# Rolling the batch loop of two stages of an attention and nearest-neighbour kernel into a counted loop on each engine

## The chip, the cores and the metric

The kernel runs on one core of a Trainium2 chip. The metric is the device time of one execution in microseconds. The engines are TensorE (PE; its weight loads are listed as PEld), VectorE (DVE), ScalarE (ACT), GpSimd (POOL) and SyncE (SP), which here only issues DMAs. Each engine has an instruction stream of its own, and they meet only through semaphores.

## The reference

Two layers run on 32 batches of 128 channels by 1024 positions.

```python
# layer 0: attention in chunks of 64 positions, 8 heads of 16 channels
q, k, v = ctx @ Wq.T + bq, ctx @ Wk.T + bk, ctx @ Wv.T + bv
out = softmax(q k^T * Dh**-0.5 + mask) v, projected by W_out, times masks, plus x
y = (out - mean) * rsqrt(var + 1e-5)              # over the 1024 positions
# layer 1: 30 nearest neighbours of each position by the first three rows of ctx
idx = top_k(2 p.p - |p|^2 - |p|^2, 30)
rel = pts[idx] - pts                              # then rho, theta, phi
h = three small linear layers with batch norm over all pairs and leaky relu
att = softmax(h, over the 30 neighbours)
result = y + sum_k y[:, idx_k] * att_k
```

(The distance in the kernel is taken over all 128 rows of ctx, as the reference's call does.)

## The kernel before

The program has three stages, each a block of its own with an all-engine meeting point at its end.

**Stage A** (`stage_a`) loops over the 32 batches. For each it takes 8 tiles of 128 positions. PE makes the distances (`pd_ps`, lines 413 and 415), ACT moves them into a ring of four tiles in SBUF (`pd_sb`), and DVE finds the 32 largest of each row in four rounds: MAX8 (line 891) finds eight, FIND_INDEX8 (line 896) their places, and MATCH_REPLACE8 (line 898) takes them out, except in the last round. Two tiles are interleaved, so that an operation on one follows an operation on the other. Beside that, PE, ACT and POOL do the chunked attention of the same batch (`s_ps`, `sS`, `kz`, `mi_ps`) and gather the coordinates of the neighbours of the batch before by products with one-hot rows: a `fill` (line 488) spreads an index code, ACT turns it into a one-hot row `ohT`, and twelve small products (line 509) fetch the coordinates. There are 60 such units for each batch. PE works two tiles ahead of DVE with the distances and one tile ahead with the scores.

**Stage B** works on the whole set of 7680 pairs a partition (spherical features, the three small layers, the batch norms). It has no loop over batches.

**Stage E** loops over the 32 batches again. Each batch has two halves (`q`, with n = 2b + q), and each half has eight groups of 16 rows. For each group DVE makes one-hot rows `e_oh` (line 1835), PE multiplies them by spread weights into `e_a_ps` (line 1907, 48 products of 32 columns), ACT copies that into `e_at` (line 1678), and PE multiplies the `e_at` of the half before by the turned rows `e_xT` into `e_o_ps` (line 1921, two products behind each group from the second on, four behind that one). DVE adds `e_o_ps` to the normalised rows (line 1822). At the head of each half PE turns the rows of the next half (line 1886), and DVE needs ACT's copy of them for `heat` (line 1791).

The order of the instructions is written out by hand in an `emit` function on each engine, which takes the batch `b`, the pair number `j` = b // 2, the parity `par` = b % 2 and two flags for the ends. Semaphores are never reset within a stage: a wait names a running total, such as `b * UNITS + q * K + k + 1`. `gate` (line 105) is a wait that is an instruction of its own, as it also counts up a semaphore; each MAX8 and each FIND_INDEX8 stands behind one or two of them. `batches` calls `emit` for each batch; it is the only thing that the change touches. In both stages it hands over plain numbers, so that all totals and addresses are constants and the program has the instructions of all 32 batches one behind the other.

```python
            for b in range(B):
                emit(b, b // 2, b % 2, b == 0, b == B - 1)
```

Of the kernel before, what the change touches and what calls it, by code (L numbers as in the profile page):

```python
# [23 lines left out]
B, C, T = 32, 128, 1024  # L24
# [123 lines left out]
def stage_a(nc, x, ctx, mask, w_in, b_in, w_out, b_out, consts, y_dram, cst, con, planes, idx_all, stats_all, sums, wts, weights):  # L148
    OHR = 3
    XR = 97  # L150
    with ExitStack() as st:
# [146 lines left out]

        def batches(eng, emit):

            for b in range(B):
                emit(b, b // 2, b % 2, b == 0, b == B - 1)

        block = st.enter_context(nc.Block())

# [1 line left out]
        def _(sp):  # L307
# [36 lines left out]
            def emit(b, j, par, first, last):  # L344
# [15 lines left out]
                sp.dma_start(y_dram[b], y_s[:].rearrange("p h t -> p (h t)")).then_inc(y_stored, 16)  # L360

            batches(sp, emit)
            sp.wait_ge(y_stored, 16 * B)
            sp.wait_ge(weights_landed, 9 * 16)

        @block.tensor
        def _(pe):
# [214 lines left out]
            queries_keys(misc0, 0, 0)  # L582
            scores(0, 0, 0)
            batches(pe, emit)
            tail = Misc(TAIL, TAIL % 2)
            probs_in = turn_probs(tail, B - 1, TILES - 1)
# [5 lines left out]
        def _(act):  # L592
# [163 lines left out]
            for t in range(2):  # L756
                for h in range(2):
                    distances(0, 0, t, h, normed)
            queries_keys(mv0, 0, 0)
            batches(act, emit)  # L760
            tail = Moves(TAIL, TAIL % 2)
            turned_probs(tail)
# [753 lines left out]
def stage_e(nc, con, planes, idx_all, stats_all, last_bn, y_dram, out):  # L1516
# [5 lines left out]
    with ExitStack() as st:  # L1522
# [71 lines left out]

        def batches(eng, emit):

            for b in range(B):
                emit(b, b // 2, b % 2, b == B - 1, b < B - 2)


        block = st.enter_context(nc.Block())
# [1 line left out]
        @block.sync  # L1603
        def _(sp):
            def load(b, par):

                if passed(b - 1):
                    gate(sp, x1_ready, b - 1, e_sp_gates)
                sp.dma_start(y_s[:, par, :], y_dram[b]).then_inc(y_landed[par], 16)

            def store(b, q):
                gate(sp, o_added, b * QUADS + q + 1, e_sp_gates)
                sp.dma_start(out[b][:, bass.ts(q, HALF)], o_s[:, q, :]).then_inc(stored[q], 16)

            def emit(b, j, par, last, further):
                if not last:
                    load(b + 1, 1 - par)
                if passed(b):
                    store(b - 1, 1)
                store(b, 0)  # L1620

            load(0, 0)
            batches(sp, emit)
            store(B - 1, 1)
            for q in range(QUADS):
                sp.wait_ge(stored[q], 16 * B)

        @block.scalar
        def _(act):
# [76 lines left out]
            logits(1)  # L1706
            exponent(1)
            batches(act, emit)

        @block.vector  # L1710
        def _(dve):
# [160 lines left out]
            for step in range(4):  # L1872
                soft(1, step)
            batches(dve, emit)
            add(B * QUADS - 2, B - 1, 0, 1)
            add(B * QUADS - 1, B - 1, 1, 1)
# [94 lines left out]
```

## Time and profile before

| | |
|---|---|
| median of 3 runs | 5462.31 us (5458.58 to 5465.13) |
| the profiled execution | 5458.58 us, of which the span is 5456.7 us |
| busy over the span | DVE 96%, PE 79%, ACT 71%, POOL 46% |
| stage A | from the start to about 3912 us, with a tail from about 3650 us on that has no loop |
| stage B | about 3912 to 4230 us |
| stage E | about 4230 us to the end |
| mean granted TensorE clock | 0.91 of full speed |

A busy share is the time in which an engine had an instruction in work. An engine that is nearly always busy in a stage sets that stage's time; idle time of another engine is slack as long as its work is there when it is needed. The time outside the span is 1.9 us.

### The profile page before, as it was taken

What the parts mean: (1) busy time and instruction counts of PE and PEld (TensorE: products, weight loads), DVE (VectorE), ACT (ScalarE), POOL (GpSimd) and SP (SyncE); (2) the same over time, 40 slices, a digit from 0 to 9 for tenths busy, and PEclk for the clock granted to TensorE, in tenths of its full rate; (3) what the DMA queues carried; (4) which work ended last, traced back from release to release, by engine and by line L of the source; (5) the groups of instructions that cost most, each with busy time, mean ns of one, the idle gap of its engine ahead of it and who ended that gap; (6) DMA issues with size and microseconds to landing.
All of it is one profiled execution on the core that took longest, in us unless ns stands there. A gap on an engine that the chain in (4) does not pass through costs nothing. (4 is left out here: it accounts for less than half of the span.)

```text
span 5456.7 us, 152862 instructions
## 1 busy us (share of the span) xinstructions
PE 4292.5 (79%) x62610; PEld 2634.9 (48%) x63182; DVE 5235.3 (96%) x7660; ACT 3871.1 (71%) x9296; POOL 2502.9 (46%) x3044
## 2 busy tenths in 40 slices
PE   5777787877777777777777777773295899999999
PEld 2444444444444444444444444442142677777776
DVE  7999999999999999999999999998998999999997
ACT  3677777777777777777777777776433777777776
POOL 3566676666766667666676666664000000000000
PEclk7899998999999999999999999996597899999999
DMA  1000000010000100001000010000000001000010
GB/s 32 17 26 23 17 17 17 17 33 17 17 17 17 33 17 17 17 17 32 17 17 17 17 33 17 17 9 5 0 0 0 32 28 32 30 32 32 28 34 26
DMA packets 135464, 112.55 MB, mean 21 GB/s; under 512 B 105328, under 2 KB 105840, under 8 KB 134640
## 3 DMA queue, kind: packets, MB, share of 16 engines
q1 hardware_dynamic: 134768, 102.73, 6.5%
q8 instruction: 502, 8.22, 0.6%
q14 instruction: 194, 1.59, 0.1%
HBM read 69.16 MB, written 33.55 MB: 19 GB/s over the span
## 5 line engine op out<-in xcount | busy, mean ns | idle before, releaser
L594 ACT ACTIVATE ohT<-oh_ps 128x512 bf16<-128x512 f32 x1920 | 1151.5, 615 | 163.0 <-PE oh_ps L488 130.1
L896 DVE FIND_INDEX8 idx<-vals,pd_sb 128x8 uint16<-128x1024 f32 x1024 | 1258.9, 1234 | 0.0
L891 DVE MAX8 vals<-pd_sb 128x8 f32<-128x1024 f32 x1024 | 1209.2, 1227 | 42.3 <-ACT pd_sb L594 42.1
L509 PEld LDWEIGHTS g_ps<-tparts,ohT 128*128 128x128 bf16 x23040 | 857.3, 98 | 358.4 <-issue 109.3
L898 DVE MATCH_REPLACE8 pd_sb<-vals,pd_sb 128x1024 f32<-128x1024 f32 x768 | 942.4, 1227 | 0.0
L509 PE MATMUL g_ps<-tparts,ohT 128*128 128x24 bf16 x23040 | 873.8, 174 | 86.6 <-issue 36.8
L1907 PEld LDWEIGHTS e_a_ps<-planes,e_oh 120*128 120x128 bf16 x24576 | 684.3, 97 | 269.6 <-issue 169.1
L733 ACT ACTIVATE sS<-s_ps,mx 128x64 f32<-128x64 f32 x2048 | 612.7, 327 | 278.8 <-DVE mx L915 278.8
L1678 ACT COPY e_at<-e_a_ps 128x512 f32<-128x512 f32 x512 | 543.9, 1062 | 302.7 <-PE e_a_ps L1907 295.7
L1907 PE MATMUL e_a_ps<-planes,e_oh 120*128 120x32 bf16 x24576 | 699.7, 177 | 58.7 <-DVE e_oh L1835 58.7
L488 PE MATMUL oh_ps<-bitsT,code 128*128 128x512 bf16 x1348 | 568.4, 426 | 216.2 <-ACT bitsT L751 127.2
L413 PE MATMUL pd_ps<-ctx_s 128*128 128x512 f32 x1024 | 616.7, 686 | 88.4 <-ACT pd_sb L594 86.5
L1113 POOL TENSOR_TENSOR sS<-sS,rs 128x512 f32<-128x512 f32 x256 | 266.7, 1042 | 808.4 <-DVE rs L919 808.3
L1835 DVE TENSOR_TENSOR e_oh<-e_pairs,e_iotan 120x2048 bf16<-120x2048 bf16 x512 | 625.6, 1223 | 0.9 <-PE e_a_ps L1907 0.9
L1040 POOL TENSOR_TENSOR gsb<-gsb 128x240 f32<-128x240 f32 (+2 forms) x1152 | 559.6, 486 | 90.3
L1137 POOL TENSOR_TENSOR kz<-kt,cst 128x1024 f32<-128x1024 f32 x256 | 486.8, 1902 | 153.3 <-ACT kt L594 146.1
L488 PEld LDWEIGHTS oh_ps<-bitsT,code 128*128 128x128 bf16 x1920 | 188.2, 101 | 757.4 <-ACT ohT L594 311.0
L1921 PE MATMUL e_o_ps<-e_at,e_xT 128*128 128x512 f32 x1024 | 548.3, 628 | 0.2 <-ACT e_at L1678 0.2
L594 ACT ACTIVATE pd_sb<-pd_ps,nxx 128x512 f32<-128x512 f32 x512 | 365.0, 713 | 207.9 <-PE pd_ps L415 207.6
L1037 POOL TENSOR_TENSOR gsb<-gsb,hi1h 128x480 f32<-128x480 f32 x384 | 442.9, 1153 | 67.3 <-ACT gsb L675 67.3
L446 PE MATMUL s_ps<-xp,negs 32*64 32x512 bf16 x512 | 113.9, 441 | 427.8 <-ACT sS L733 421.1
L733 ACT ACTIVATION_READ_ACCUMULATOR sS<-s_ps,mx 128x1 f32 x2048 | 450.1, 220 | 0.0
(277 smaller groups left out, 6700.6 us busy)
## 6 DMA issues: line engine op xcount, KB each, us to landing
ctx_s<-in_ctx SPq DMA_DIRECT2D x32, 512.0 KB, 4.9
maskb<-in_mask_Bx1x_ff SPq DMA_DIRECT2D x32, 512.0 KB, 6.3
x_s<-in_x SPq DMA_DIRECT2D x32, 512.0 KB, 5.7
y_spill<-y_s SPq DMA_DIRECT2D x32, 512.0 KB, 3.0
e_y<-y_spill SPq DMA_DIRECT2D x32, 512.0 KB, 4.1
out<-e_o SPq DMA_DIRECT2D x64, 256.0 KB, 2.5
table<-in_ctx SPq DMA_DIRECT2D x96, 4.0 KB, 5.9
pd_sb<-in_shape_constants SPq DMA_DIRECT2D x1, 1024.0 KB, 5.2
```

The lines of the kernel that those rows point to most:

```text
L413: nc.tensor.matmul(pd_ps[:], ctx_s[:, par, bass.ts(t, P)], ctx_s[:, par, bass.ts(h, HALF)], start=True, stop=False)
L488: nc.tensor.matmul(oh_ps[k % 2][:], code[:, k % KT, :], bitsT[:, k // KT, :], start=True, stop=True).then_inc(oh_ready, 1)
L509: m = nc.tensor.matmul(found_ps[gi % 2][:, k % GK, t, :], ohT[:, k % OHR, bass.ts(t, P)], tparts[:, par, part, :], start=(part == 0), stop ...
L594: return nc.scalar.activation(dst, src, func, scale=scale, bias=bias)
L733: m = nc.scalar.activation(sS[:, t % 2, hd, :], s_ps[:, hd, :], ACT.Exp, bias=mx[:, t % 2, hd:hd + 1], accum_out=rs[:, t % 2, hd:hd + 1])
L891: nc.vector.max(vals[:, i, :], pd_sb[:, (t + i) % RING, :]).then_inc(topk_step, 1)
L896: found = nc.vector.max_index(idx16[:, par, t + i, 8 * r:8 * r + 8], vals[:, i, :], work)
L898: nc.vector.match_replace(work, vals[:, i, :], work, REMOVED).then_inc(topk_step, 1)
L1040: steps(nc.gpsimd.tensor_tensor(sums[:, :, 0:width], sums[:, :, 0:width], sums[:, :, width:2 * width], ALU.add))
L1835: v.tensor_tensor(oh[pp, g % RING], low.to_broadcast([QCOLS, NB // 2, LO, 2]), row.to_broadcast([QCOLS, NB // 2, LO, 2]), ALU.is_equal).th ...
L1907: m = nc.tensor.matmul(a_ps[g % 2][:, i].rearrange("p t e -> p (t e)"), oh[pp, g % RING, i // 2, :, i % 2], spr[q][pp, part, :, (g * NB + ...
L1921: m = nc.tensor.matmul(o_ps[q][:], xT[:, par, e, :], at[:, q, e].rearrange("p t n -> p (t n)"), start=(e == 0), stop=(e == HI - 1))
```

## The change

Both `batches` functions keep the first two and the last two batches as they were, and put the 28 between them into a counted loop (`Fori`) of 14 passes on each engine, with two batches in its body. The body's `b` is now 2j or 2j + 1 with j in a register, so wherever `emit` computes a total to wait for, or an address with `b` in it, the value is worked out from the register while the program runs. Tile parities stay constants. Where `emit` or a helper of it asks whether `b` is a plain number (for the first batches, where there is nothing to wait for yet), a register counts as "not a plain number". At the end of each pass every engine adds one to its own counter, compares and branches back; no engine waits there for another, and no hint for the fetching of the branch's target is given. The instructions of the engines, their order, the buffers and the DMAs are the same.

```diff
@@ stage_a
         def batches(eng, emit):
 
-            for b in range(B):
-                emit(b, b // 2, b % 2, b == 0, b == B - 1)
+            emit(0, 0, 0, True, False)
+            emit(1, 0, 1, False, False)
+            with eng.Fori(1, B // 2 - 1) as j:
+                emit(j * 2, j, 0, False, False)
+                emit(j * 2 + 1, j, 1, False, False)
+            emit(B - 2, B // 2 - 1, 0, False, False)
+            emit(B - 1, B // 2 - 1, 1, False, True)
@@ stage_e
         def batches(eng, emit):
 
-            for b in range(B):
-                emit(b, b // 2, b % 2, b == B - 1, b < B - 2)
+            emit(0, 0, 0, False, True)
+            emit(1, 0, 1, False, True)
+            with eng.Fori(1, B // 2 - 1) as j:
+                emit(j * 2, j, 0, False, True)
+                emit(j * 2 + 1, j, 1, False, True)
+            emit(B - 2, B // 2 - 1, 0, False, False)
+            emit(B - 1, B // 2 - 1, 1, True, False)
```

## Rows read from the trace of the kernel before

**Rows 1.** Busy time of each engine by stretch: stage A, stage E, one batch of each.

```profile
core 0: us, PE busy (x) PEld busy (x) DVE busy (x) ACT busy (x) POOL busy (x), PEclk, DMA share, GB/s
120.00:3650.00 3530.00, 2756.91 (x34389) 1592.86 (x34936) 3508.11 (x5220) 2646.02 (x7844) 2368.28 (x2901) 0.91 0.07 20
4300.00:5300.00 1000.00, 960.55 (x21758) 716.08 (x21754) 916.99 (x1515) 749.29 (x801) 0.00 (x0) 1.00 0.09 31
...
1523.90:1638.30 114.40, 88.64 (x1104) 51.41 (x1122) 113.60 (x171) 85.92 (x255) 77.57 (x95) 0.91 0.08 20
4733.60:4771.20 37.60, 36.14 (x819) 26.92 (x818) 34.50 (x57) 28.14 (x31) 0.00 (x0) 1.00 0.09 31
```

**Rows 2.** Waits in stage E, 4300 to 5300 us: us in total, times, longest.

```profile
PE e_a_ps L1907 <- DVE e_oh L1835: 39.5, 54, 1.0
```

**Rows 3.** The page: instructions in all, and the DMA queues.

```profile
PE 4292.5 (79%) x62610; PEld 2634.9 (48%) x63182; DVE 5235.3 (96%) x7660; ACT 3871.1 (71%) x9296; POOL 2502.9 (46%) x3044
...
q8 instruction: 502, 8.22, 0.6%
q14 instruction: 194, 1.59, 0.1%
```

**Rows 4.** DMA issues: size and us from issue to landing.

```profile
y_spill<-y_s SPq DMA_DIRECT2D x32, 512.0 KB, 3.0
...
cst<-in_shape_constants SPq DMA_DIRECT2D x1, 294.0 KB, 2.9
...
bias<-in_L_xattn_b_out SPq DMA_DIRECT2D x1, 0.5 KB, 5.0
```

**Rows 5.** DVE in order of time at the end of a batch of stage A.

```profile
1636.01 2.33 DVE L891 MAX8 vals<-pd_sb 128x8 f32<-128x1024 f32 x2
1638.26 0.07 DVE L896 MATCH_VALUE_LOAD idx<-vals,pd_sb 128x8 f32 x1
1638.32 1.22 DVE L896 FIND_INDEX8 idx<-vals,pd_sb 128x8 uint16<-128x1024 f32 x1
```

**Rows 6.** Instructions of the sequencers, by line: duration min/median/max in ns.

```profile
L108 DVEq EVENT_SEMAPHORE  x2334: 21/21/21569, 11.7 to 3712.9; - x195
```

```profile
L1904 PEldq EVENT_SEMAPHORE  x510: 51/51/51, 4250.5 to 5442.5; - x170
```

```profile
L1207 DVEq COMPARE_BRANCH  x1: 57/57/57, 4229.1 to 4229.1; - x1
```

**Rows 7.** PE in order of time around the end of a batch of stage E (at 4733.62).

```profile
4731.46 1.37 PE L1907 MATMUL e_a_ps<-planes,e_oh 120*128 120x32 bf16 x48
4732.68 1.10 PE L1921 MATMUL e_o_ps<-e_at,e_xT 128*128 128x512 f32 x2
4733.62 0.44 PE L1886 MATMUL e_pr_ps<-e_identb,e_rowsb 128*120 128x128 bf16 x5
4733.90 1.36 PE L1907 MATMUL e_a_ps<-planes,e_oh 120*128 120x32 bf16 x48
4736.29 1.37 PE L1907 MATMUL e_a_ps<-planes,e_oh 120*128 120x32 bf16 x48 [1.02 <-DVE e_oh L1835]
```

**Rows 8.** DVE in order of time over the same end of a batch.

```profile
4731.44 0.83 DVE L1810 TENSOR_SCALAR planes<-e_wgt,cst 120x1024 bf16<-120x1024 bf16 x2
4732.18 1.22 DVE L1835 TENSOR_TENSOR e_oh<-e_pairs,e_iotan 120x2048 bf16<-120x2048 bf16 x1
4733.82 0.69 DVE L1822 TENSOR_TENSOR e_o<-e_o_ps,e_x 128x512 f32<-128x512 f32 x1 [0.42 <-PE e_o_ps L1921]
...
4735.01 1.22 DVE L1835 TENSOR_TENSOR e_oh<-e_pairs,e_iotan 120x2048 bf16<-120x2048 bf16 x1
```

## Prediction, made before the changed kernel ran

> **What bounds the kernel now.** I read the busy time by stretch first. In stage A DVE is busy 3508 of 3530 us, 99.4%, while in one batch of 114.4 us PE idles 25.8 us, ACT 28.5 us and POOL 36.8 us [rows 1]. So DVE sets stage A, and whatever makes DVE's queue run dry there is paid in full, while the other three have slack. In stage E it is the other way round: PE is busy 960.6 of 1000 us and DVE 917.0 [rows 1]. PE sets stage E, and nearly all of what it waits for is DVE's one-hot rows, 39.5 us in 54 waits over 1000 us [rows 2]. Stage B and the tail of A have no loop over batches; the change leaves them alone.
>
> Then I looked at what feeds the engines. The page lists DMA queues of the kind "instruction": 502 packets with 8.22 MB and 194 with 1.59 MB [rows 3]. 8.22 MB over 62,610 matmuls and 63,182 weight loads is 65 bytes each, so the first queue carries PE's program in blocks of 16.4 KB, some 250 instructions. The other carries the rest in blocks of 8.2 KB, about 128 instructions at the same size. The programs are thus read in while they run. In a straight program the next block is always known; at a branch back it is an old one.
>
> **The size of a pass.** One batch of stage A has 1104 + 1122 instructions on PE, 171 on DVE, 255 on ACT, 95 on POOL; one of stage E has 819 + 818 on PE, 57 on DVE, 31 on ACT [rows 1]. A pass is two batches, so its body is about 18 PE blocks in A and 13 in E, and on DVE 342 instructions and its gates in A (2334 gates over 32 batches are 73 a batch [rows 6]), some 490 or four blocks, against about one in E. Fori(1, 15) makes 14 passes, so each loop has 13 taken branches on each engine.
>
> **What a taken branch costs.** No taken branch back stands in the trace. The compare-and-branch itself is small: one took 57 ns [rows 6]. What matters is whether its target must be fetched again. A block's packet keeps a DMA engine for 0.6% x 16 x 5456.7 / 502 = 1.04 us [rows 3], which is the lower bound of a fetch. The upper one is the slow read of 0.5 KB, 5.0 us from issue to landing [rows 4]. I take 3.0 us, after the plainest single transfers, 2.9 and 3.0 us [rows 4].
>
> The Trainium skill ("Runtime: NRT & Kernel Launch", section Instruction fetch mechanics) says that a taken branch whose target isn't in the instruction memory forces a fetch before anything goes on, and that PE holds 2048 instructions, the others 512. By that rule PE misses in both stages, DVE and ACT can miss in A, and the small bodies of E and of POOL need not. The trace agrees with the blocks of 16 KB for PE, not for the other queue, whose blocks are 8.2 KB; whether a block is kept, no row here shows.
>
> **Term 1, DVE in stage A.** The branch can be covered only by work already queued. The gate ahead of the last FIND_INDEX8 opens when the second MAX8 ends, at about 1638.3; from there DVE has two finds of 1.22 us [rows 5], 2.4 us in all, and the last one's issue takes some 0.2 us of that, so 2.2 us cover the branch. Against it stand 3.0 us of fetch and about 0.5 us for counter, compare, and the waits at the head of the next batch with their register values (a gate is 21 ns, a branch 57 ns [rows 6]; the register instructions are not in the trace). The stall is 1.3 us, times 13 = **16 us**. From both sides: 0 us (fetch 1.04), and (5.0 + 0.5 - 2.2) x 13 = 43 us. The branches of PE, ACT and POOL in stage A I cost at nothing: some 3 us every 229 us against a slack of 50 us or more on each; the distances are two tiles ahead of DVE in a ring of four. If that cover were gone they would cost up to 3 x 13 = 39 us.
>
> **Term 2, PE in stage E.** When PE's sequencer has issued the last group, the two products of line 1921 (0.94 us from 4732.68 to 4733.62) and part of the 48 pairs (1.22 us for all of them) are still ahead [rows 7]. How many are queued the trace doesn't show, so the cover is 0.94 to 2.2 us; I take 1.7. The stall is 3.0 + 0.3 - 1.7 = 1.6 us. Some of it comes back: in the second group after the boundary PE waits 1.02 us for `e_oh` [rows 7], because DVE's add at 4733.82 had waited for PE, and `e_oh` at 4735.01 stands behind it [rows 8]. During the stall DVE gets that done, unless its own branch, which stands ahead of the `e_oh` at 4732.18, holds it up. I count half of the 1.02 us. 1.1 us x 13 = **14 us**. From both sides: 0, and (5.0 + 0.3 - 0.94) x 13 = 57 us. Behind a stalled PE stand turn_pairs, ACT's copy and DVE's `heat`; they shift with PE and add nothing of their own.
>
> **Term 3, the arithmetic for the waits.** By the code PE waits about 210 times a batch in stage A and 48 times in E (16 groups twice, 6 before line 1921, 4 and 4 at the heads, 2 for the turning). Each value now comes from a register. The trace has no such instruction; the nearest row is a semaphore instruction on PE's sequencer, 51 ns [rows 6]. In stage A one more of that a wait is 10.7 us a batch, under the 25.8 us of slack: nothing. DVE's operations of 1.2 us cover several such instructions each. In stage E 48 x 51 ns x 28 batches = 69 us if all of it shows, 0 if none does. Six groups of eight have the 0.94 us of line 1921 behind them, in which the sequencer has four instructions to issue and can run ahead. Only the heads (a quarter of the waits, 17 us) have no such cover, and there PE waits for DVE anyway. I take half, **9 us**. Dynamic addresses on SP's DMAs, on POOL's writes to `planes` and on ACT's logits lie on engines with slack in both stages; they cost nothing, at most what POOL's slack leaves.
>
> **Sum.** 16 + 14 + 9 = 39 us on the profiled execution's 5458.6 us gives 5497.6 us. The median of the runs is 3.7 us above that execution, so I predict 5501 us. What a measurement of this kernel can tell from no change is 0.2%, 11 us.
>
> **Rivals.**
> *It costs nothing.* If a block comes back in under 1.7 us, or is kept, DVE's 2.2 us and PE's 1.7 us cover it, and terms 1 and 2 vanish. For it: a packet is only 1.04 us long, and the sequencers are ahead at just these places. Against it: no transfer of this kernel lands in so little. Time 5462 to 5468 us. It decides from a fetch of 1.7 us down. The Trainium skill ("Advanced Engine Details and Errata", section Control Flow Timing) gives a compare-and-branch about 108 ns and nothing further; by that alone the branches would come to an estimated 3 us over both stages.
> *The arithmetic shows in stage E.* PE has no slack there, and if the sequencer isn't ahead of the array, each wait costs at least its 51 ns: +69 us with one instruction a wait, +138 us with two. With 30 us for the branches that is 5561 to 5630 us. For it: PE idles only 4% [rows 1]. Against it: the 0.94 us behind most groups.
> *PE becomes the bound of stage A.* Three instructions a wait, 0.153 us x 210 = 32 us a batch, pass its slack of 25.8 us by 6 us, times 28 = 177 us; with all else about 5700 us. It decides from 25.8 / 210 = 0.12 us a wait. Against it: much of the arithmetic falls into time in which PE waits for ACT anyway.
> *Faster.* A body small enough to be kept needs no fetches; only POOL's and SP's can be, and neither bounds. 5445 us at best.
>
> **Chances.** Forecast (5474 to 5550) 0.57; costs nothing 0.17, of which 0.01 falls on the faster side; arithmetic in E 0.16; PE bound in A 0.07; faster 0.03. The range 5464 to 5600 us takes in the forecast, most of the second case and three quarters of the third; it leaves out the last two. Faster by over 0.2% 0.03, within 0.2% 0.16, slower 0.81.
>
> **What would show it.** In the changed profile: DVE in stage A with a gap of about 1.3 us ahead of the MAX8 at the head of each second batch, 13 times, and no other new gaps; the time of a batch inside the loop as before, 114.4 us. In stage E a gap of 1 to 2 us on PE ahead of line 1886 in every second batch, a batch otherwise at 37.6 us. The instruction queues keep their size or grow a little. It would be wrong if the batches inside a pass themselves get longer (the arithmetic shows), if the waits of PE for ACT in stage A vanish and DVE waits for `pd_sb` or `s_ps` (PE is the bound), or if the gaps at the branches are absent, or 4 us and more.

## The result, and the profile after

The changed kernel takes 5558.80 us (median of 4 runs, 5556.25 to 5561.41) against 5461.78 us before: a ratio of 1.0177 [1.0160, 1.0196], 97 us slower. The forecast was 5501 us. The direction and the range (5464 to 5600) hold; the size is 2.5 times the forecast one.

I split the spans of the two profiled executions (5456.7 and 5560.9 us) by the starts of two operations. From DVE's first FIND_INDEX8 to its last, stage A's search, it is 3651.4 us before and 3673.4 after, +22.0. From the first `e_oh` to the last, stage E, it is 1190.1 and 1270.2 us, +80.1. What lies between grows by 1.4 us. So four fifths of the loss is in stage E, where I had put 23 of 39 us.

The page of the changed kernel, busy time and instruction queues [rows 3]:

```profile
span 5560.9 us, 167643 instructions
PE 4439.9 (80%) x63182; PEld 2657.8 (48%) x63182; DVE 5241.2 (94%) x7660; ACT 3864.8 (69%) x9296; POOL 2499.9 (45%) x3044
...
q8 instruction: 566, 9.27, 0.7%
q14 instruction: 320, 2.62, 0.2%
```

The busy time of DVE, ACT and POOL is as before to 0.2%; PE's is 147 us larger. Only 27 us of that lie in stage E (1159.4 us before, 1186.1 after), and they are, as will be seen, products that took longer. The rest lies in stage A and is mostly a matter of records: 572 products are missing from the trace of before, and the trace of e7 below, which has them all and whose stage A is that of before, shows 118 us more there, too. Over 60 more blocks came through PE's instruction queue, and 126 more through the other: something is fetched again. (A block of PE's queue holds some 250 instructions by [rows 3].)

The two loops' own instructions by line (duration min/median/max in ns), the first two from stage A, the others from E [rows 6]:

```profile
L303 DVEq COMPARE_BRANCH  x14: 55/63/63, 492.4 to 3486.8; - x14
L303 PEldq COMPARE_BRANCH  x14: 83/3820/4472, 494.6 to 3490.2; - x14
...
L1604 PEldq FUSED_REGOPS  x14: 59/59/64, 4343.2 to 5397.3; - x14
L1604 PEldq ALU_OP  x14: 32/32/32, 4419.7 to 5475.3; - x14
L1604 PEldq COMPARE_BRANCH  x14: 79/3702/3864, 4419.8 to 5475.4; - x14
```

PE's branch is recorded with the wait for its target inside it: 3.7 us in E, 3.8 in A, and 0.08 us the one time in 14 that it isn't taken. The other engines' branches are recorded as about 0.05 us, and the wait, if any, follows: in A the next instruction that DVE's sequencer takes after its branch at 1873.8 comes 2.8 us later, ACT's 2.6 to 3.8 and POOL's 2.6 to 2.9 us later, in E DVE's comes about 0.27 and ACT's about 0.24 us later. The Trainium skill ("Runtime: NRT & Kernel Launch", Instruction fetch mechanics) has it that a taken branch stalls for a fetch where the target is not held; the trace agrees for PE in both stages and DVE, ACT and POOL in A, while DVE and ACT in E, with small bodies, show no fetch. With the sequencers' own instructions counted, a pass has 643 recorded instructions on DVE, 787 on ACT and 428 on POOL in A, and 201 on DVE and 118 on ACT in E.

PE in order of time around one of these branches, the one at 4905.8 [rows 7]. In brackets stands the idle time before a group and what ended it; `issue` means that the engine waited for nothing that the profile shows, so its next instruction simply came late:

```profile
4906.05 1.10 PE L1931 MATMUL e_o_ps<-e_at,e_xT 128*128 128x512 f32 x2
4909.77 0.78 PE L1896 MATMUL e_pr_ps<-e_identb,e_rowsb 128*120 128x128 bf16 x5 [2.61 <-issue]
4910.35 1.06 PE L1917 MATMUL e_a_ps<-planes,e_oh 120*128 120x32 bf16 x32
4913.48 1.87 PE L1917 MATMUL e_a_ps<-planes,e_oh 120*128 120x32 bf16 x64 [2.08 <-issue]
4915.19 3.76 PE L1931 MATMUL e_o_ps<-e_at,e_xT 128*128 128x512 f32 x4
4918.75 1.42 PE L1917 MATMUL e_a_ps<-planes,e_oh 120*128 120x32 bf16 x48
```

From the start of the two products of line 1931 to the group behind the four it is 12.70 us; before it was 6.63 (4732.68 to 4739.31; the first rows of that stretch are in [rows 7], the last two are these):

```profile
4737.51 1.96 PE L1921 MATMUL e_o_ps<-e_at,e_xT 128*128 128x512 f32 x4
4739.31 0.86 PE L1907 MATMUL e_a_ps<-planes,e_oh 120*128 120x32 bf16 x28
```

The 6.07 us are made up as follows, each from start to start. The turning comes 2.78 us late. It takes 0.58 us for 0.28: +0.30. The two groups behind it take 4.84 us for 3.61: a second gap of 2.08 us, from which the standing wait for `e_oh` of 1.02 us, which has gone, comes off, and 0.17 us of slower products: +1.23. The four products of line 1931 take 3.56 us for 1.80: +1.76.

The granted clock of the same place (PEclk is the third column from the right, full speed is 1.00):

```profile
core 0: us, PE busy (x) PEld busy (x) DVE busy (x) ACT busy (x) POOL busy (x), PEclk, DMA share, GB/s
4902.00:4908.60 6.60, 5.16 (x108) 3.58 (x105) 5.83 (x13) 5.11 (x7) 0.00 (x0) 1.00 0.01 2
4908.60:4912.60 4.00, 1.64 (x37) 1.56 (x38) 2.86 (x5) 0.69 (x1) 0.00 (x0) 0.52 0.53 195
4912.60:4918.90 6.30, 5.42 (x72) 3.16 (x72) 6.30 (x12) 2.12 (x2) 0.00 (x0) 0.50 0.02 7
4918.90:4940.00 21.10, 20.66 (x497) 15.55 (x495) 15.03 (x23) 14.97 (x16) 0.00 (x0) 1.00 0.05 16
```

From 4908.8 on, inside the first gap, TensorE has its lower level, 1.2 GHz, for 10.2 us, and pays in whatever runs there. In the 13 places the four products take 2.6 to 3.55 us, 3.2 in the mean, 18 us in all over 1.80 each; that, and the smaller groups beside them, makes up the extra busy time of PE in E.

PE's longest waits in stage E, 4300 to 5400 us (us in total, times, longest) [rows 2]:

```profile
PE e_pr_ps L1896 <- issue: 33.1, 13, 2.7
PE e_a_ps L1917 <- issue: 29.7, 12, 4.0
PE e_a_ps L1917 <- DVE e_oh L1845: 28.5, 42, 1.1
```

The first gap stands there 13 times and the second 12 times, 62.8 us together; the thirteenth second gap, 2.6 us at 5401.7, lies past the window. A batch with a branch ahead of it takes 43.5 us in the mean, the other one of a pair 37.7; both took 37.6 before. 5.95 us x 13 = 77 us.

In stage A, DVE at the end of a pass [rows 5], and its waits from 494 to 3490 us, first after, then before:

```profile
1873.48 1.22 DVE L901 FIND_INDEX8 idx<-vals,pd_sb 128x8 uint16<-128x1024 f32 x1
1874.62 0.07 DVE L901 MATCH_VALUE_LOAD idx<-vals,pd_sb 128x8 f32 x1
1874.67 1.22 DVE L901 FIND_INDEX8 idx<-vals,pd_sb 128x8 uint16<-128x1024 f32 x1
1877.12 2.35 DVE L896 MAX8 vals<-pd_sb 128x8 f32<-128x1024 f32 x2 [1.22 <-issue]
```

```profile
DVE vals L896 <- issue: 17.2, 13, 1.5
DVE vals L896 <- ACT pd_sb L599: 13.5, 20, 1.3
```

```profile
DVE vals L891 <- ACT pd_sb L594: 14.0, 24, 1.1
```

There is the gap that was forecast: two finds cover the branch, and 1.2 to 1.5 us stick out, 13 times.

### The profile page after: what moved, and what is told of

The parts are those of the page before. It is cut to its first block and busy times, and to the rows that moved or that the text cites. A ratio compares the mean times of both kernels' runs of the same rounds, so it can differ in the third digit from the quotient of the medians.

```text
span 5560.9 us, 167643 instructions
## 1 busy us (share of the span) xinstructions
PE 4439.9 (80%) x63182; PEld 2657.8 (48%) x63182; DVE 5241.2 (94%) x7660; ACT 3864.8 (69%) x9296; POOL 2499.9 (45%) x3044
## 3 DMA queue, kind: packets, MB, share of 16 engines
q14 instruction: 320, 2.62, 0.2%
## 5 line engine op out<-in xcount | busy, mean ns | idle before, releaser
L901 DVE FIND_INDEX8 idx<-vals,pd_sb 128x8 uint16<-128x1024 f32 x1024 | 1245.1, 1219 | 0.0
L493 PE MATMUL oh_ps<-bitsT,code 128*128 128x512 bf16 x1920 | 811.1, 429 | 223.6 <-ACT bitsT L756 132.8
L903 DVE MATCH_REPLACE8 pd_sb<-vals,pd_sb 128x1024 f32<-128x1024 f32 x768 | 928.8, 1209 | 0.0
L418 PE MATMUL pd_ps<-ctx_s 128*128 128x512 f32 x1024 | 645.4, 716 | 77.9 <-ACT pd_sb L599 76.5
L1931 PE MATMUL e_o_ps<-e_at,e_xT 128*128 128x512 f32 x1024 | 568.2, 649 | 0.2 <-ACT e_at L1688 0.2
```

What stands on the lines that cost most here:

```text
L418: nc.tensor.matmul(pd_ps[:], ctx_s[:, par, bass.ts(t, P)], ctx_s[:, par, bass.ts(h, HALF)], start=True, stop=False)
L493: nc.tensor.matmul(oh_ps[k % 2][:], code[:, k % KT, :], bitsT[:, k // KT, :], start=True, stop=True).then_inc(oh_ready, 1)
L901: found = nc.vector.max_index(idx16[:, par, t + i, 8 * r:8 * r + 8], vals[:, i, :], work)
L903: nc.vector.match_replace(work, vals[:, i, :], work, REMOVED).then_inc(topk_step, 1)
L1931: m = nc.tensor.matmul(o_ps[q][:], xT[:, par, e, :], at[:, q, e].rearrange("p t n -> p (t n)"), start=(e == 0), stop=(e == HI - 1))
```

## The experiments

In each, a stage that isn't named is as in the changed kernel. "A as before" or "E as before" means that this stage's `batches` is the plain loop over all 32 batches. Ratios are to the kernel before on the same chip.

**Does the register arithmetic cost anything?** One pass for each `Fori`, so that all 14 pairs of batches are written out, each with its `b` from a register, and no branch is taken:

```diff
-            with eng.Fori(1, B // 2 - 1) as j:
+            for jj in range(1, B // 2 - 1):
+              with eng.Fori(jj, B // 2 - 1, B) as j:
```

> All 28 batches of each stage stand one behind the other again, each pair in a counted loop of its own that is left after one pass: 13 of the 14 pairs still work their wait values and addresses out of a register, and no branch is taken. Theory F (the cost is the fetching behind a taken branch, on TensorE in stage E two fetches in a row, then a lower clock): within 0.2% of before, at most +11 us, a batch of stage E at 37.6 to 37.7 us. Theory R (the register arithmetic holds TensorE up): most of the change's 97 us stays, +60 us or more.

Measured: 5461.70 us, 0.9995 [0.9986, 1.0004]. The time can't be told from before, so the loss is in the taken branches. In E the arithmetic is small, but not nothing: a batch takes 37.68 us for 37.58, and two of them 39 us. PE's waits there, 4300 to 5400 us, before and then e1:

```profile
PE e_a_ps L1907 <- DVE e_oh L1835: 42.8, 59, 1.0
PE e_a_ps L1919 <- DVE e_oh L1847: 44.9, 58, 1.1
```

The wait for `e_oh` at each boundary is 1.11 us for 1.02. It comes from DVE: its add into `e_o` starts 1.74 us after the `e_oh` ahead of it for 1.64, behind a register instruction of 46 ns that stands between PE's result and the add. e7 below, where PE has no register at all, has the same 1.74, 1.11 and 37.67 us.

**Which stage?** A rolled with E as before, and E rolled with A as before.

> Only stage A is rolled, stage E is as before. Theory F: DVE loses 1.2 us at each of 13 branches, 16 us, and a few us more where TensorE and ScalarE come late with a tile: +15 to +28 us. Theory R: stage A has slack on all engines but DVE, so no more than a few us: under +11 us. A rival of mine that the stages cost about the same would have +48 us.

> Only stage E is rolled, stage A is as before. In the changed kernel's trace every second batch of E is about 5.9 us longer, 13 times, so 77 us; but TensorE's loop head now stands at another place in its fetch block, since the program ahead of it is longer. Theory F with two fetches in a row: between +40 us (a whole block stands behind the head, one gap of about 2.5 us) and +90 us (the head near a block's end). Theory R: +75 us wherever the head is.

Measured: 5477.94 us, 1.0029 [1.0018, 1.0040], +13.5; and 5564.77 us, 1.0178 [1.0162, 1.0193], +100. The two are more than the change has together, and e3 lies above the +40 to +90 us expected. In e3 the stage E body begins at another place of its block. PE there:

```profile
4734.81 1.10 PE L1926 MATMUL e_o_ps<-e_at,e_xT 128*128 128x512 f32 x2
4739.26 0.78 PE L1891 MATMUL e_pr_ps<-e_identb,e_rowsb 128*120 128x128 bf16 x5 [3.35 <-issue]
4743.69 2.74 PE L1912 MATMUL e_a_ps<-planes,e_oh 120*128 120x32 bf16 x96 [3.64 <-issue]
4746.27 3.22 PE L1926 MATMUL e_o_ps<-e_at,e_xT 128*128 128x512 f32 x4
```

The second gap stands after 5 products here, where it stood after 37 in the changed kernel, and is 3.6 us where it was 2.1. So it isn't tied to an operation or a wait of the kernel.

**Is the second gap the block behind the target?** If PE gets only the block that holds the target, its length behind the target decides. E rolled, A as before, the head of PE's loop body placed at slot 0 or 232 of a block (the slot is an instruction's place in its block):

```diff
-            with eng.Fori(1, B // 2 - 1) as j:
+            with eng.bass.Fori(1, B // 2 - 1, engines=[eng.engine],
+                               head_slot={eng.engine: 0} if eng.engine == mybir.EngineType.PE else None) as j:
```

> Only stage E is rolled, and TensorE's loop head is put at slot 0 of a fetch block of 256, so that a whole block stands behind the branch's target. Theory F: the second gap behind each branch (2.1 us in the changed kernel, after 32 of 48 products of the first group) is gone and the clock falls less: an excess of 2.5 to 4 us for a branch, +33 to +52 us. A rival, that the second gap is a wait for DVE or ScalarE, has it unchanged: +75 us.

> As the kernel with only stage E rolled, but TensorE's loop head at slot 232 of its fetch block: 24 slots stand behind the branch's target before the next block. Theory F (the block after the target is a second fetch in a row, and its wait is the longer, the fewer instructions stand before it): a gap behind the first group's opening products, an excess of 6 to 8 us for a branch, +80 to +105 us, and over 25 us more than with the head at slot 0. A rival, that only the one fetch of the target counts and the head's place changed something else: the same +56 us as at slot 0.

Measured: slot 0 5520.44 us, 1.0103 [1.0088, 1.0119], +56; slot 232 5547.20 us, 1.0151 [1.0135, 1.0167], +82; the first is 4 us above its expected range. With slot 0, PE after a branch:

```profile
4721.79 0.78 PE L1892 MATMUL e_pr_ps<-e_identb,e_rowsb 128*120 128x128 bf16 x5 [3.36 <-issue]
4722.37 2.77 PE L1913 MATMUL e_a_ps<-planes,e_oh 120*128 120x32 bf16 x96
4724.98 2.85 PE L1927 MATMUL e_o_ps<-e_at,e_xT 128*128 128x512 f32 x4
```

The second gap is gone and 44 of e3's 100 us with it; the lower clock stays (96 and four products in 5.3 us for 4.2). With slot 232 the gap is back after some 9 products. In the three traces with a second gap (the changed kernel, e3 and e5) the instructions behind it start 3.1 to 5.5 us after the branch ends, as late as a fetch that starts with the branch's end. With slot 0 PE comes to that place only 5.9 us or more after the branch and waits for nothing.

**What if the target is fetched ahead?** Both stages as in the changed kernel, with an instruction at the head of each body that names the target of the branch at its end:

```diff
-            with eng.Fori(1, B // 2 - 1) as j:
+            with eng.bass.Fori(1, B // 2 - 1, engines=[eng.engine], hint_back_edge=True) as j:
```

> Both stages rolled as in the change, and each loop carries a hint for the fetch of its branch's target, set at the head of each pass. Theory F: the target's block is there when the branch comes, the branch is short on every engine, and the stall ahead of line 1886 and of DVE's MAX8 goes: 0 to +25 us over before, what is left being the block behind the target if the hint brings one block alone (up to 2 to 3.6 us for a TensorE branch in E, then +25 to +50 us). If the branches stay at 3.7 us, the hint doesn't work for so long a body and nothing is learned of the cost: +97 us.

Measured: 5470.09 us, 1.0006 [0.9997, 1.0015]. 93 of the 97 us are gone. The hint and the branch of PE in E:

```profile
L1604 PEldq BRANCH_PREFETCH_HINT  x14: 36/36/40, 4318.2 to 5305.6; - x14
L1604 PEldq COMPARE_BRANCH  x14: 88/354/364, 4393.6 to 5382.1; - x14
```

In E 3.7 us have become 0.35, in A 3.8 have become 1.8. DVE's next instruction in A comes 0.5 us after its branch for 2.8, its gaps there are gone, and it waits 7.7 us for `pd_sb` in the stretch where it waited 14.0 before. The block behind the target still comes late (0.91 us of `issue` after 36 products at 4702.5), about where the wait for `e_oh` stood. The hint has a price where the loop ends: behind the last branch, which isn't taken, PE stands 2.62 us at 5386.8, with `issue` again, after 22 products.

**Is it PE alone in E?** E with PE's program straight and those of DVE, ACT and SP rolled, A as before:

```diff
+            if eng.engine == mybir.EngineType.PE:
+                for b in range(B):
+                    emit(b, b // 2, b % 2, b == B - 1, b < B - 2)
+            else:
...
+                with eng.Fori(1, B // 2 - 1) as j:
```

> Stage A as before; in stage E TensorE keeps the straight program and the four others run the counted loop. Theory F (all of stage E's excess is TensorE's): within 0.2% of before. A rival, that the branches of DVE and ScalarE share in it: +20 us or more.

Measured: 5469.54 us, 1.0007 [0.9998, 1.0016]. All but a few us of E's loss are PE's. The stage E of this trace is 6.8 us longer than before, in the way of e1: 0.1 us a batch and three batches of 39 us.

**Which engine in A?** E as before; in A DVE straight and the rest rolled (e8), DVE alone rolled (e9), PE alone rolled (e10), each with an `if eng.engine == ...` as above.

> Stage E as before; in stage A DVE keeps the straight program, the four others run the counted loop and take 2.6 to 4 us for each branch. My term 1 (only DVE's own branch costs, the rest is slack): within 5 us of before, and the excess of 13.5 us of the kernel with only stage A rolled is gone. A rival, that the late distances behind TensorE's and ScalarE's branches cost the most of it: +8 us or more stays.

> Only DVE runs the counted loop, and only in stage A; the rest is as before. If DVE's own branch costs by itself what its gaps show (1.2 us, 13 times), +12 to +20 us. If it is hidden by waits that DVE would have had anyway (14 us in 24 waits for the distances in the loop's stretch before), under +6 us.

> Only TensorE runs the counted loop, and only in stage A. Theory P (the late distances, 31.5 us of DVE's waits with DVE straight against 14.0 before, come from TensorE's two fetches in a row): +7 to +15 us. A rival, that ScalarE's branch (2.6 to 3.9 us) is what makes them late: under +4 us.

Measured: e8 5476.87 us, 1.0021 [1.0012, 1.0030], +11; e9 5477.77 us, 1.0020 [1.0011, 1.0029], +13; e10 5492.69 us, 1.0050 [1.0036, 1.0064], +28. DVE's waits from 494 to 3490 us in e9, e8 and e10:

```profile
DVE vals L900 <- issue: 16.3, 13, 1.4
DVE vals L900 <- ACT pd_sb L603: 12.7, 17, 1.5
```

```profile
DVE vals L900 <- ACT pd_sb L603: 31.5, 32, 2.5
```

```profile
DVE vals L900 <- ACT pd_sb L603: 45.4, 33, 2.5
```

e9 is the forecast case: DVE's own branches, 16 us, and the waits for `pd_sb` as before. e8 and e10 are misses: with no branch of its own, DVE waits 17 and 31 us more for `pd_sb`. In e10 PE's branch alone reaches DVE, through the distances. The parts don't add: 13 (DVE) and 11 (all others) make 13.5 together in e2, as the engines stop at the same time. That PE alone (e10) costs more than PE, ACT and POOL together (e8) I can't explain; the branches of ACT and POOL were not taken alone.

**Half as many branches.** Both stages, four batches a pass (`Fori(1, B // 2 - 2, 2)`, with `emit` of j * 2 + 2 and j * 2 + 3 added): 6 taken branches for 13.

> Both stages rolled with four batches in a pass, so 6 taken branches instead of 13 on each engine in each stage. Theory F (the cost goes with the number of branches, about 6 us each in E with TensorE's head where it stood, 3 to 8 us by its place, and 1 to 1.5 us in A): +30 to +60 us. Theory R (the cost goes with the batches whose waits are worked out): +90 us or more.

Measured: 5502.45 us, 1.0066 [1.0051, 1.0082], +37.5. By the count 97 x 6 / 13 = 45 us. The loss goes with the number of branches. The longer bodies also show what the smaller engines hold. In E, DVE's pass now has 399 recorded instructions, and after its branch the next one comes 3.4 to 3.6 us later, where 201 had shown no fetch; ACT's, with 233, still comes after 0.24 us.

**Hint and slot together.** As e6, with the head of PE's body in E at slot 0 (e12); and E alone rolled, A as before, the hint on PE alone, with no slot named (e13):

```diff
+            with eng.bass.Fori(1, B // 2 - 1, engines=[eng.engine], hint_back_edge=True,
+                               head_slot={eng.engine: 0} if eng.engine == mybir.EngineType.PE else None) as j:
```

> The hint in both stages, and TensorE's loop head in stage E at slot 0. With the hint alone TensorE still stands 1.1 to 1.6 us after the first 37 products of a pass in E, where the second block is awaited, and some batches are 39 us. With a whole block behind the head this gap should go: every second batch of E at 37.7 us, and the time within 0.1% of before; no version can be faster than before by this theory.

> Stage A as before, stage E rolled on all engines, the hint on TensorE alone. If TensorE's branch carries all of stage E's loss, as with the hint on every engine: 0 to +15 us against +100 us without it. If the branches of DVE and ScalarE matter once TensorE's is short: +20 us or more.

Measured: 5495.36 us, 1.0052 [1.0039, 1.0066], +30; and 5498.86 us, 1.0060 [1.0044, 1.0075], +34. Both are misses: I had expected the two remedies to add. PE's branch in E, e12 and then e13:

```profile
L1604 PEldq COMPARE_BRANCH  x15: 88/2720/3127, 4319.4 to 5409.2; - x15
```

```profile
L1599 PEldq COMPARE_BRANCH  x14: 88/2688/3175, 4400.1 to 5413.0; - x14
```

2.7 us in both, for 0.35 in e6. (There are 15 in e12 because placing the head adds a jump ahead of the loop; in E it took 0.33 us.) In e13, too, over 100 products follow the branch before any later block is missing, so its head lies near the start of a block. There the hint doesn't bring the target in time. Both have a second loss, at places with no branch. PE at one of them in e12, and the clock of it:

```profile
4905.31 1.40 PE L1918 MATMUL e_a_ps<-planes,e_oh 120*128 120x32 bf16 x48 [1.11 <-DVE e_oh L1846]
4906.55 3.57 PE L1932 MATMUL e_o_ps<-e_at,e_xT 128*128 128x512 f32 x4
```

```profile
4907.00:4911.00 4.00, 4.00 (x46) 1.90 (x46) 4.00 (x7) 0.79 (x1) 0.00 (x0) 0.65 0.09 35
4911.00:4920.00 9.00, 9.00 (x214) 6.72 (x211) 9.00 (x17) 7.07 (x8) 0.00 (x0) 1.00 0.01 4
```

The wait for `e_oh` is 1.11 us there for 1.02 before, and behind it the clock falls to half for 3.4 us. Four products that take over 2 us instead of 1.80 stand at 20 places of e12, 12 of them with no branch near, and at those they lose 1.1 to 1.7 us (11 of the 12 behind a wait of 1.11 us, one behind 1.02); e13 has 18 and 10, e6 has 8 in all, e1 has 2. The kernel before has none, but the length of the wait alone doesn't decide it: e2, e9, e10, e14 and e15, with the stage E of before, have one each behind the same 1.02 us.

**The hint in A, and the slot in A.** A rolled on all engines with the hint on PE alone (e14); A with PE alone rolled, its head at slot 0 (e15); E as before.

> Stage E as before, stage A rolled on all engines, the hint on TensorE alone. If the own branch of DVE is what costs in A (a gap of 1.2 us 13 times): +12 to +18 us, as with all unhinted. If DVE's gaps only stand in for waits that TensorE's late distances would make: under +8 us.

> Only TensorE runs the counted loop, in stage A, with its head at slot 0 of a fetch block. If the second fetch behind the branch (about 4 us) is what makes the distances late: +5 to +18 us, clearly under the +27.7 us without it. If it is the first fetch or the waits' arithmetic: +25 us or more.

Measured: 5471.07 us, 1.0012 [1.0003, 1.0021], +6 (e2: +13.5); and 5483.71 us, 1.0035 [1.0022, 1.0049], +19 (e10: +28). The +19 lies between the two expected ranges, and its interval touches both, so how much the second fetch has in A stays undecided. In e14 DVE's own gaps stay:

```profile
DVE vals L897 <- issue: 16.7, 13, 1.4
DVE vals L897 <- ACT pd_sb L600: 5.4, 8, 0.8
```

DVE waits 22.1 us in these two, 8 more than the 14.0 of before, and the run pays 6. So DVE's branch is partly paid out of waits for `pd_sb` that it had anyway, as long as PE isn't late too.

**Where must the head lie for the hint to work?** As e13, with the head at slot 174 or 100.

> As e13 (only stage E rolled, the hint on TensorE alone), with TensorE's loop head at slot 174, about where the changed kernel has it by the 82 instructions ahead of its second gap; the branch then stands some 216 slots into its block. If the hinted fetch only starts with the block that holds the branch, it has time: the branch takes 0.4 us as in e6, the time is 0 to +12 us over before. If e6 was better because the hint stood on all engines: branches of 2.7 us and +30 us again.

> As e16 with the head at slot 100: 156 instructions behind the target, the branch some 142 slots into its block. By the same theory both waits shrink or go, the branch is under 1.5 us and the 1.1 us gap behind the first 82 instructions is gone: 0 to +12 us, not slower than at slot 174 by more than 5 us.

Measured: slot 174 5475.52 us, 1.0012 [1.0003, 1.0021]; slot 100 5471.35 us, 1.0006 [0.9997, 1.0015]. e16 has the hint on PE alone and still the short branch of e6, so it is the position that decides, not the hints of the other engines. PE's branch, slot 174 and then 100:

```profile
L1599 PEldq COMPARE_BRANCH  x15: 88/357/385, 4332.0 to 5393.3; - x15
```

```profile
L1599 PEldq COMPARE_BRANCH  x15: 88/799/1114, 4329.7 to 5387.1; - x15
```

PE at the branch at 4783.0 of the second:

```profile
4784.27 0.48 PE L1893 MATMUL e_pr_ps<-e_identb,e_rowsb 128*120 128x128 bf16 x5
4784.59 1.36 PE L1914 MATMUL e_a_ps<-planes,e_oh 120*128 120x32 bf16 x48
4786.99 1.37 PE L1914 MATMUL e_a_ps<-planes,e_oh 120*128 120x32 bf16 x48 [1.04 <-DVE e_oh L1842]
```

That is the picture of [rows 7]: no gap at the branch is left. With the hint the branch lasts 2.7 us at slot 0, 0.8 at 100 and 0.36 at 174.

The parts of all spans side by side, from the first to the last FIND_INDEX8 (A) and from the first to the last `e_oh` (E), and the median of PE's branches:

| kernel | median us | A us | E us | PE branch A, E us |
|---|---|---|---|---|
| before | 5461.78 | 3651.4 | 1190.1 | none |
| changed | 5558.80 | 3673.4 | 1270.2 | 3.8, 3.7 |
| e1, no branch taken | 5461.70 | 3645.9 | 1195.3 | 0.07, 0.08 |
| e2, A rolled | 5477.94 | 3667.2 | 1191.5 | 3.8, none |
| e3, E rolled | 5564.77 | 3658.5 | 1289.9 | none, 4.8 |
| e4, E, slot 0 | 5520.44 | 3653.4 | 1246.7 | none, 4.6 |
| e5, E, slot 232 | 5547.20 | 3654.9 | 1272.5 | none, 3.4 |
| e6, hint | 5470.09 | 3648.9 | 1206.8 | 1.8, 0.35 |
| e7, E, PE straight | 5469.54 | 3659.6 | 1196.9 | none |
| e8, A, DVE straight | 5476.87 | 3669.9 | 1190.9 | 3.8, none |
| e9, A, DVE alone | 5477.77 | 3670.8 | 1191.5 | none |
| e10, A, PE alone | 5492.69 | 3685.3 | 1191.8 | 3.8, none |
| e11, four batches a pass | 5502.45 | 3660.5 | 1228.4 | 3.6, 3.6 |
| e12, hint, slot 0 in E | 5495.36 | 3649.7 | 1229.3 | 2.0, 2.7 |
| e13, E, hint on PE | 5498.86 | 3655.8 | 1228.2 | none, 2.7 |
| e14, A, hint on PE | 5471.07 | 3663.5 | 1191.4 | 1.7, none |
| e15, A, PE alone, slot 0 | 5483.71 | 3672.4 | 1191.6 | 3.5, none |
| e16, E, hint, slot 174 | 5475.52 | 3662.2 | 1201.6 | none, 0.36 |
| e17, E, hint, slot 100 | 5471.35 | 3659.8 | 1197.7 | none, 0.8 |

In e3, e4, e5, e7, e13, e16 and e17 stage A is that of before, and still its length is 2 to 11 us more. It goes with the granted clock: the profiled execution of before had a mean clock of 0.910, those of e7, e16 and e17 had 0.898 to 0.901, and DVE waits 19.5 to 20.8 us for `pd_sb` there for 14.0. Within one kernel it is the same: the five runs of e17 at 0.907 to 0.909 took 5468.2 to 5470.2 us, the six at 0.898 to 0.901 took 5471.4 to 5476.5. Why the clock differs from run to run I don't know; it bounds what can be read into a few us in A. No version is faster than the kernel before.

## Why the prediction was right or wrong

**What bounds the kernel**: held for E, where all but a few us are PE's (e7). In A DVE sets the time, but PE's program reaches it (e10); whether ACT's and POOL's alone would, no run shows.

**Term 1, 16 us for DVE in stage A**: the gap was right, 1.3 us forecast and 17.2 us in 13 measured (1.3 x 13 is 17, not the 16 of the forecast). Its terms fit too: a fetch of 2.8 us for 3.0, 0.5 us behind it, 2.1 us of cover. That the 3.0 us fit DVE is luck: they were taken from transfers of 294 and 512 KB, and PE's own fetch was 3.7. With DVE alone rolled it costs 12.8 us (e9). The step "the branches of PE, ACT and POOL in stage A I cost at nothing" failed. I had measured their slack over a whole batch and taken "two tiles ahead" for cover; with DVE straight they cost 11 us (e8), PE's alone 28 (e10). In the change itself little of it shows, as they stop together with DVE: the stage as a whole costs 13.5 us (e2).

**Term 2, 14 us for PE in stage E**: this is the step that failed, 77 us measured. A stall of 1.6 us was forecast, less 0.5 us given back. Its parts at 4905.8:
- the fetch was 3.7 us, not 3.0, and its cover 1.2 us (from the branch at 4905.8 to the end of the two products at 4906.99), not 1.7. That makes a gap of 2.8 us, a term mis-sized by 1.2 us.
- a second gap of 2.1 us, the block behind the target. I had reckoned with one fetch a branch. e3, e4 and e5, which move only the head, move this gap from 37 products to 5, to none and to 9. 
- the lower clock, some 2 us. I had written that what stands behind a stalled PE shifts with it and adds nothing. It adds, because PE's own products become slower: 1.76 us in the four of line 1931, 0.30 in the turning.
- the return was 1.0 us, all of the standing wait and not half.

2.8 + 2.1 + 2.1 - 1.0 = 6.0 us. With the fetch, the cover and the return put right and nothing else, term 2 would have been (3.7 + 0.3 - 1.2 - 1.0) x 13 = 23 us: the two effects that I had not thought of make the difference. The upper bound of this term, 57 us, was too low for the same reason. The forecast's own range ended at 5550 us; the wide one held only because the rivals about the arithmetic had widened it.

**Term 3, 9 us for the arithmetic**: nothing that the whole time shows, -2.7 us with an interval of about 5 either way (e1). The batches of E show 0.1 us each, 3 us over 28, and they come from DVE and not, as forecast, from PE's waits. The ALU_OP of 32 ns and the FUSED_REGOPS of 59 ns on PE's sequencer are as large as the 51 ns assumed; e7, which has none of them, is no faster in E, so the sequencer had the time.

**The rivals.** "It costs nothing" falls with the branch of 3.7 us, above the 1.7 from which it decides. Both rivals about the arithmetic fall with e1: batches inside a pass keep their 37.7 us, and PE doesn't become the bound of A. "Faster" falls. It counted on POOL's small body, but with the sequencer's own instructions that is 428 a pass, and it was fetched anew each time. The bodies of DVE and ACT in E are held, and nothing is won by that. The 512 instructions that the prediction took for these engines aren't borne out: 201 and 233 are held, 399 and 428 are not. The sentence that the forecast would be wrong if the gaps were "4 us and more" names what happened: the two gaps together are 4.7 us.

**Shown and not shown.** That the loss comes from PE's fetches at the branch in E is shown by e1 (no branch), e7 (PE straight), e11 (half of them), e4 and e5 (position) and e6 and e16 (fetched ahead). That the lower clock costs time is read from rows at both levels; no run took it away alone. Open are why the median branch without a hint is 3.4 to 4.8 us long in the different kernels, why a hint with the head near the start of a block leaves 2.7 us, and why PE alone costs more in A than all engines without DVE.

## What to carry to other kernels

A rolled loop costs next to nothing for its register arithmetic here (0.1 us a batch of E), but on an engine whose body exceeds what it holds (201 instructions a pass were held on DVE, 399 were not; 428 were not on POOL), each taken branch costs the fetch less what is queued ahead of it, and then again for the next block if little of the target's block is left. On PE add the slower clock behind the gap. Look at the engine that bounds the stage: either keep its program straight and roll the others (e7, +0.07%), or fetch the target ahead and place the head some way into its block (e6, e17, +0.06%), and compare both against the number of passes.

## What was unexpected of the hardware

- PE's taken branch holds its sequencer 3.3 to 5.0 us; on DVE, ACT and POOL in stage A the next instruction comes 2.6 to 3.8 us later, on DVE, ACT and SP in E, and on SP in A, after 0.16 to 0.33 us.
- The fetch at a branch of PE brings the block of the target only. The instructions of the next one come 3.1 to 5.5 us after the branch, after 5, 9 or 37 products by the place of the target in its block; with the target at slot 0 nothing waits for it.
- What DVE, ACT and POOL hold is small: passes of 201 (DVE) and 233 (ACT) instructions were run again without a fetch, passes of 399 (DVE) and 428 (POOL) cost 2.6 to 3.6 us each time.
- A prefetch of the target shortens PE's branch to 0.35 us, or to 0.8 or 2.7 us, by the position of the target in its block (slots 174, 100, 0).
- TensorE's clock fell to half for about 10 us behind gaps of 2.6 and 2.1 us with 37 products between them, and for about 3 us behind a single wait of 1.11 us at 11 places of e12. The wait of 1.02 us at the same operation had that effect nowhere in the kernel before, and at one place in each of five kernels with the same stage E. The Trainium skill ("TensorE: Matmul & The Clock Gate", HAM oscillation) tells of such a loop, in which the fall of the clock is paid again in every round; the rows here agree, with gaps shorter than those of its example.
- Stage A was 2 to 11 us longer than before in seven kernels in which its code is the same, and the longer, by and large, the lower the granted clock.
